# Attention scores as float32 products in 32-row strips, in place of stacked bf16 parts

## The reference

```python
x = x + gamma * attention(layernorm(x), ctx)     # x, ctx: (16, 64, 256)
x = x + ffn(layernorm(x))
# attention: 8 heads of 8 rows each; per batch and head, q, k: [8, 256]
qk  = einsum('dq,dl->ql', q, k) / sqrt(8)        # k = v = ctx, 256 x 256 scores
ret = einsum('ql,dl->dq', softmax(qk, -1), v)
# ffn: activations rounded to 8 bits, weights to -1/0/1, width 256 -> 1024 -> 256
h = silu(bit_linear(x, w_gate)) * bit_linear(x, w_up)
y = bit_linear(rms_norm(h) * ln_weight, w_down)
```

## Time and profile before

| | |
|---|---|
| runs, us | 245.23, 247.96, 244.26 |
| median | 245.23 |
| span of the profiled execution | 248.6 |
| PE, DVE, ACT, POOL busy | 178.4, 151.6, 140.9, 107.3 |

### The profile page before, as it was taken

The page is one execution under the profiler, slowest core; times in us unless marked ns, Lnnn a source line. Parts: engine busy times, 40 slices in busy tenths (PEclk is TensorE's granted clock), DMA queues, the critical chain, the costliest instruction groups (busy, mean ns, idle before and its releaser), DMA issues.

```text
span 248.6 us, 4308 instructions
## 1 busy us (share of the span) xinstructions
PE 178.4 (72%) x1370; PEld 103.8 (42%) x1378; DVE 151.6 (61%) x282; ACT 140.9 (57%) x286; POOL 107.3 (43%) x282
## 2 busy tenths in 40 slices
PE   0006331972988958994999799589979998893793
PEld 0002111540666624662466366245745664441432
DVE  2105840563297974985666989736886769436273
ACT  4110000893466845973568599447856587975432
POOL 3630310406624544734652586436435226626240
PEclk9999999996599997997569999965995699999689
DMA  3599599348201450253026314601540000000000
GB/s 100 139 142 261 126 177 313 115 121 154 63 1 37 118 107 0 56 149 77 1 67 141 75 26 116 135 9 34 142 105 0 5 3 22 7 21 0 22 1 21
DMA packets 15871, 19.95 MB, mean 80 GB/s; under 512 B 2649, under 2 KB 14057, under 8 KB 14697
## 3 DMA queue, kind: packets, MB, share of 16 engines
q1 hardware_dynamic: 15321, 18.89, 31.8%
q10 hardware_dynamic: 528, 0.79, 1.4%
HBM read 15.20 MB, written 4.19 MB: 78 GB/s over the span
## 4 chain that ended last, share of the span: by engine, by line
PE 33%; DMA 14%; DVE 7%; issue 6%; ACT 6%; POOL 4%; SPq 3%; POOLq 0%; ACTq 0%; DVEq 0%
DMA q_stack<-mt 13%; PE psO L463 9%; PE psB L447 7%; PE psA L433 6%; PE psG L565 2%; PE psG L505 2%; ACT probs L594 2%; PE psG L555 2%; POOL hw L325 2%; DVE mneg L736 1%; SPq L333 1%; ACT o_sb L629 1%; SPq L341 1%; DVE wgT L755 1%; DVE w_sb L747 1%
## 5 line engine op out<-in xcount | busy, mean ns | idle before, releaser
L736 DVE TENSOR_REDUCE mneg<-psA 128x2 f32<-128x512 f32 x128 | 82.7, 680 | 46.5 <-PE psA L433 46.4
L594 ACT ACTIVATE probs<-psB 128x512 f32<-128x512 f32 x128 | 74.0, 597 | 39.8 <-PE psB L447 39.7
L433 PE MATMUL psA<-k_stack,q_stack 72*128 72x256 bf16 x256 | 57.9, 319 | 23.1 <-DMA q_stack<-q_scratch 20.7
L447 PE MATMUL psB<-q_stack,k_stack 75*128 75x256 bf16 x256 | 55.2, 303 | 23.8 <-DMA q_stack<-mt 22.0
L463 PE MATMUL psO<-probs,vt 128*32 128x256 f32 x512 | 41.6, 451 | 1.0 <-ACT probs L594 1.0
L433 PEld LDWEIGHTS psA<-k_stack,q_stack 72*128 72x128 bf16 x256 | 23.9, 108 | 43.3 <-issue 30.1
L447 PEld LDWEIGHTS psB<-q_stack,k_stack 75*128 75x128 bf16 x256 | 25.7, 108 | 37.2 <-DMA q_stack<-mt 23.8
L325 POOL TENSOR_TENSOR hw<-h,lnw 128x512 f32<-128x512 f32 x15 | 19.1, 1270 | 39.3 <-DVE h L826 28.0
L463 PEld LDWEIGHTS psO<-probs,vt 128*32 128x32 f32 x512 | 14.8, 121 | 16.9 <-issue 9.9
L815 DVE SCALAR_TENSOR_TENSOR gu<-th,psG 128x512 f32<-128x512 f32 x15 | 10.3, 688 | 9.7 <-ACT th L657 9.7
L657 ACT ACTIVATE th<-psG,tscale 128x512 f32<-128x512 f32 x15 | 10.3, 688 | 9.1 <-PE psG L535 9.0
(11 more groups left out here) (129 smaller groups left out, 268.4 us busy)
## 6 DMA issues: line engine op xcount, KB each, us to landing
q_stack<-q_scratch SPq DMA_DIRECT2D x24, 192.0 KB
k_stack<-k_scratch SPq DMA_DIRECT2D x21, 192.0 KB
q_scratch<-q_parts SPq DMA_DIRECT2D x24, 64.0 KB, 2.1
k_scratch<-k_parts SPq DMA_DIRECT2D x21, 64.0 KB, 2.0
w_sb<-in_L_ffn_w_gate_dram SPq DMA_DIRECT2D x4, 256.0 KB, 8.0
w_sb<-in_L_ffn_w_up_dram SPq DMA_DIRECT2D x4, 256.0 KB, 7.5
w_sb<-in_L_ffn_w_down_dram SPq DMA_DIRECT2D x4, 256.0 KB, 4.1
out_dram<-y_sb SPq DMA_DIRECT2D x8, 128.0 KB, 4.2
```

The costliest lines, as they stand in the source:

```text
L433: mm = pe.matmul(psA[n % A_BANKS][:, qt * L:(qt + 1) * L], q_stack[0:STACK, t % NBUF, bh, qt * P:(qt + 1) * P], k_stack[0:STACK, t % NBUF, ...
L447: mm = pe.matmul(psB[b % 2][:, lt * L:(lt + 1) * L], k_stack[:, t % NBUF, bh, lt * P:(lt + 1) * P], q_stack[:, t % NBUF, bh, :], start=Tru ...
L594: act.activation(probs[:, b % RING, :], psB[b % 2][:, :], ACT.Exp, scale=SCALE).then_inc(s_exp, 1)
L736: dve.tensor_reduce(mneg[:, k % MBUF, QT * (bh % HALF):QT * (bh % HALF + 1)], psA[n % A_BANKS][:, :].rearrange("p (q l) -> p q l", q=QT), ...
```

## The change

There are no stacks and no parts. `q` holds the normalised x in float32, in two copies (`half` 0 and 1), each masked to half of the heads' rows. `cm` holds ctx in float32 in four copies (`j` 0 to 3), each with all rows zero but the 8 of one head in every 32-row strip, and 8 rows that hold a one for the maxima. Both products of a unit contract over one 32-row **strip** of the array (`STRIP` = 32) in float32. A unit n uses strip (n mod 8) // 2, and with `LAG` = 12 product B of the same step uses another strip than product A. Within a step PE's order is A, B, A, B (the two halves of each), behind one group of waits for both banks.

The maxima need no split: PE transposes `mneg` in float32 once for every 4 units (`quad_at` for `half_at`), ACT copies, SP sends 4 rows of 256 into `q`. Stores to DRAM and stack loads go; `cm` for tiles 1 to 7 is cleared by DVE, POOL and ACT once and filled from ctx by 16 transfers at the start; for tile 0 ACT makes it from the loaded ctx. The weights and what is left of x and ctx are issued by ACT at the start and no longer by SP between the tiles. The table of half-steps is moved by some steps throughout.

```diff
-LAG = 14
+LAG = 12
...
-        def load_k(eng, t):
...
-        def load_q(eng, t):
...
+        def clear_cm(eng, j):
+            return eng.tensor_scalar(cm[:, j, 1:T, :], zero[:, 0:1].unsqueeze(2).to_broadcast([P, T - 1, L]), mask[:, one_row(j):one_row(j) + 1], None, ALU.add)
...
+            for j in (0, 2, 1, 3):
+                sp.wait_ge(s_init[j], 1)
+                for i in range(P // STRIP):
+                    rows = slice(STRIP * i + DH * j, STRIP * i + DH * (j + 1))
+                    sp.dma_start(cm[rows, j, 1:T, :], ctx_rows[1:T, rows].rearrange("g p l -> p g l")).then_inc(s_cm[j], DMA)
...
-                    for qt in range(QT):
-                        mm = pe.matmul(psA[n % A_BANKS][:, qt * L:(qt + 1) * L],
-                                       q_stack[0:STACK, t % NBUF, bh, qt * P:(qt + 1) * P],
-                                       k_stack[0:STACK, t % NBUF, bh, :], start=True, stop=True)
-                    mm.then_inc(s_a, 1)
...
+                        if n >= A_BANKS:
+                            pe.wait_ge(s_red, n - A_BANKS + 1)
+                        first = (q[rows, t, half, :], cm[rows, j, t, :])
+                    if 0 <= b < N:
...
+                        if r % GROUP == 0:
+                            pe.wait_ge(s_mrow[r // GROUP], DMA * (2 * t + half + 1))
+                        if b >= 2:
+                            pe.wait_ge(s_exp, b - 1)
+                        second = (cm[rows, j, t, :], q[rows, t, half, :])
                     for qt in range(QT):
+                        if first:
+                            mm = pe.matmul(psA[n % A_BANKS][:, qt * L:(qt + 1) * L], first[0][:, qt * P:(qt + 1) * P],
+                                           first[1], start=True, stop=True)
...
+                        if second:
+                            mm = pe.matmul(psB[b % 2][:, qt * L:(qt + 1) * L], second[0][:, qt * P:(qt + 1) * P],
+                                           second[1], start=True, stop=True)
...
-                k = half_at(m, PE_M)
+                k = quad_at(m, PE_M)
...
-                    pe.wait_ge(s_ms, k + 1)
-                    pe.transpose(banks[BANK_M][0:PARTS * HALF * QT, 0:P // 2].bitcast(BF16),
-                                 m_parts[:, k % 2].rearrange("p c n -> p (c n)"), ident_b[:, :]).then_inc(s_mt, 1)
+                    pe.wait_ge(s_red, GROUP * (k + 1))
+                    pe.transpose(banks[BANK_M][0:GROUP * QT, 0:P], mneg[:, k % MBUF, :], ident[:, :]).then_inc(s_mt, 1)
```

More of the change, by code:

```diff
@@ L216, in build @@
         s_lnw = sem("lnw_loaded")
-        s_rows = sem("rows_of_ones_made")
         s_ident = sem("ident_made")
+        s_mask = sem("masks_made")
+        s_init = [sem(f"cm_cleared{j}") for j in range(4)]
+        s_cm0 = sem("first_cm_made")
+        s_cm = [sem(f"cm_loaded{j}") for j in range(4)]
         s_const = sem("const_made")
@@ L395, in _ @@
+            for m in range(2 * FIRST, 2 * LAST):
+                k = quad_at(m, ACT_M)
                 if k is not None:
[L396 removed]
+                    t, rest = divmod(k, 4)
+                    half, par = divmod(rest, 2)
+                    first = P // 2 * par + DH * (1 - half)
                     sp.wait_ge(s_mtsb, k + 1)
[L398 to L399 removed]
+                    sp.dma_start(q[first:first + P // 2 - DH:2 * DH, t, half, :].rearrange("p (q l) -> p q l", q=QT),
+                                 mt[:, k % 2, :]).then_inc(s_mrow[k % 2], DMA)
```

346 lines of the change are left out of this document (116 added, 230 removed).

## The result

| | before | changed |
|---|---|---|
| runs, us | 245.23, 247.96, 244.26, 250.49 | 309.08, 308.42, 304.48, 321.71 |
| median | 246.59 | 308.75 |
| span of the profiled execution | 248.6 | 307.3 |

The profiled execution of the changed kernel is the one of 309.08 us. The ratio is 1.252, with a 95% interval of 1.216 to 1.288. The forecast was 249 us with a range to 280: outside, and on the wrong side of "no change".

What follows compares the result with a forecast made beforehand. PE was taken to bound the kernel between holes. First `o_sb` at 43, tile 1 31.6, five tiles of 26.2 and a last of 24.0 reach 229.6; with 22.5 after, span 252.1, times 0.986: 249 us, range 229 to 280.

Steps and rivals of the forecast that it cites:

- on a cold clock at first: Start: twelve steps with product A alone, 0.85 to 1.7 us each, taken as 1.05; first B at 19 us.
- if PE then never idles: Tiles: condition for the half clock to go with the 7.8 us transfers, some 6 us a tile together.
- over 45 us a tile: Tiles: length at half clock if 32-row products don't hold the clock; named as making the forecast wrong, given no chance.
- `cm` arrives late: Start: sign that the forecast is wrong, `cm` coming late beside 3 MB of weights in the same engines.
- The tile's sum: One tile on PE: work 22.2 us, 13.65 of it strips (16 x 0.853), shape changes 2.3, waits 1.7; together 26.2.
- a change of shape 0.10: Tile on PE: each switch between strips and other work costs 0.10 us, 23 of them 2.3 us a tile.
- Rival 1: Tiles: shape changes and new waits are covered, 23.7 us a tile, 231 us in all; chance 0.24.
- Rival 2: Steps: the common wait in front makes ACT the pacer, +3.3 us a tile, 274 us; chance 0.20.
- Rival 3: Steps: strips don't overlap, 356 us, or loads don't, a step of 1.41 and 319 us; chance 0.10 together.
- between the holes PE is the bound: Kernel before: without holes and half clock, 16.5 to 17.3 us a tile of work that PE paces.
- the start's 28 us: Start: 28 us won there, then spent at 3.5 to 4 us a tile; break-even is a tile of 25.7 us.
- 0.986: Whole kernel: factor from span to time, turning the forecast span of 252.1 into 249 us.

Runs made afterwards that it cites:

- e6: Changed kernel with product B's waits put behind the step's first product A; 311.95 us, one run.
- e1: Changed kernel with both products contracting over 64 rows in place of 32 (output differs); 285.35 us against 308.75.
- e8: Changed kernel with both the repaired start and products over 64 rows (output differs); 278.96 us, two runs.
- e15: Kernel with the repaired start and 64-row products, made exact by zeros in the other strip's rows of q; 280.89 us, ratio 1.155 to the kernel before.
- e10: Changed kernel with both products contracting over all 128 rows, operands all from cm (output differs); 356.48 us, one run.
- e2: Changed kernel with 36 unread bf16 filler products of 128 rows on PE ahead of the first product; 315.10 us, two runs.
- e4: Changed kernel with its start repaired: ACT issues weights inside its loop, POOL and ACT share clearing cm; 302.78 and 324.59 us.
- e13: Kernel before with product B 18 steps behind product A in place of 14; 240.38 us against 249.77, repeated 243.36 against 246.65 (ratio 0.991).
- e14: Kernel with the repaired start, products of units 0 to 23 over 64 rows and later ones over 32; 335.96 us, one run.
- e3: Changed kernel with a step's products written in the order A, A, B, B; 303.06 us, two runs.
- e5: Kernel before with the transfer of the maxima issued from ACT's queue in place of SP's; 252.53 us against 247.5, ratio 1.024.
- e11: Kernel before with the maxima sent from ACT's queue and the stack loads issued one at a time; 263.14 us against 248.86.

## Why the prediction was wrong

**The step that failed is the clock.** The sum of the start and of every tile was made at full clock, apart from a first product "on a cold clock at first", and the half clock was counted among what the change removes "if PE then never idles". In the kernel before the clock does fall beside the ends of holes: at 94.8, 115.3 and 163.0 us, where the transfers of the maxima landed at 93.8, 116.5 and 162.5. In the changed kernel PE did hardly idle (42.84 busy of 43.10 us) and ran at half clock all the same (629 ns a product, against 374). e6 shows full clock lost under 32-row products with hardly a pause, e1, e8 and e15 show it won within 2 to 5 us of the first product B with 64 rows and kept through the tiles but for two falls of 3.4 us in e1, e10 with 128. I had named that condition as what would make the forecast wrong, and given it no chance among the cases: nothing in the trace of before had products over so few rows, which was a reason for a rival, not for leaving it out. My price for it, over 45 us a tile, wasn't put to the test, since no middle tile ran at half clock throughout; the stretches that nearly did took 43.1 us for a forecast 24, and in e2 and e6 39.8 and 39.6 for the last tile's 24.0.

**The size of it.** 28 to 30 us of the 55 are given back by 64 rows together with the start (e8, e15). The rest, 24.7 us in e8, is 8.7 for the stretch of products A alone at half clock, 6.5 in the first two tiles, 7.0 for five tiles that are 1.4 us longer each (0.8 to 0.9 with 32 rows), and 2.5 at the two ends.

**The start.** "`cm` arrives late" was not it. Two waits I had at nothing: POOL's 4.82 us for a copy of `cm` in front of the reciprocal root (I had named only DVE's copy, at 1.1 to 2.1; it took 2.07), and ACT held in issuing weights. Both were in the order of the changed kernel. With both gone in e4, the first B comes 5.5 us earlier.

**The tile's sum was near.** 26.2 forecast, 27.0 to 27.1 measured at full clock. Of its terms: a step 0.853, measured 0.86; a change of shape 0.10, measured about 0.10 in the gap, and a further 0.105 from the first record of a step to its next (0.32 against 0.21 us), which I had not. That stands only behind a change, so in some 11 of the 16 steps, 1.2 us, more than the 0.8 that is missing: some other term was a little too large, and I haven't tested them apart. Last tile 24.0, measured 24.1.

**Rival 1** (changes covered) didn't come. **Rival 2** (ACT as the pacer) was too big by ten times, e6. **Rival 3** (no overlap of strips, or of loads): false on both counts. The loads last 0.18 us each at full clock and stand under running products of the same strip (in the changed kernel a load of A's from 112.72 to 112.90 us, under the product of A that starts at 112.61 and lasts 0.48). A step takes 0.86 us, not the 1.41 that a load of 0.14 behind each record would have given.

**What was removed.** Right: the waits for the transfer are gone. But e13 shows that they could be had for less, by the lead, with the cheap bf16 products kept: a step's products take PE 0.44 us there against 0.86 in strips. It also shows a second step of the prediction to be wrong, "between the holes PE is the bound": a tile with neither holes nor half clock lasts 21.2 us, not 16.5 to 17.3, so there were not some 6 us a tile to win but 1.3 to 1.7. This was not in the sum for the changed kernel, which was made from PE's work alone. That the 13.65 us a tile of strips are more than even the 6 us stood in it; I let the start's 28 us weigh against them.

**The scale.** 0.986 joined the median of three runs to the span of another. In the changed kernel the profiled execution took 1.8 us more than its span, so the forecast span of 252.1 stands for 254 us; that is 5 of the 60 us by which the forecast missed.

**Open.** What starts a fall of the clock in the middle of a run of 32-row tiles (184.1 us, in e6 at 252.1) and not in others, with the same work in each; e14, e2, e3 and e4 each have four or five such tiles in a row at full clock. Between the profiled runs only the place of the falls differs, and each version was profiled once. And whether 32-row products can be kept at full clock for good by more 128-row work among them; the middle tiles, with their outputs' products and transposes, suggest it, and no experiment isolates it.

## What to carry to other kernels

Price a row strip at the clock that it will have: here products over 32 of the 128 rows ran at half clock (629 ns each) for the first 65 us, PE busy for 42.84 of the last 43.10 before the first `o_sb`, and the same products over 64 rows, half of them zeros, at full clock (376 ns) from 3 us after the first B. Before a change that removes a wait at the cost of PE's time, try to give the wait a longer lead; `LAG` and the numbers that follow from it did that here, but check what stands at the new place, since 17 steps lost where 18 won. Read the duration of one kind of product beside the clock column, above all ahead of the first change that the column shows. And before counting a wait as time to be won, find out what would bound the stretch without it.

## What the runs showed of the hardware that I had not expected

- Rows count for the clock even where a factor is zero in them (e15 against e4: 376 against 629 ns at 35 to 65 us).
- PE isn't bound to program order between row strips: A, A, B, B runs as A, B, A, B (27.2 against 27.0 us a tile). Products over 32 and over 64 rows, in contrast, don't overlap, and take 0.62 us for one product, where A and B side by side take 0.43 for both (e14).
- Products A of two units on different strips overlap too: at half clock, where records of one strip start 0.427 us apart (e2 at 12.6 to 13.8 us) and four of them would be 1.7, a unit with A alone takes 1.5 us over 32 rows (12 units in 25.3 - 7.5, e4). Over 64 it takes 1.8 (28.9 - 7.7, e8).
- An engine that issues large transfers can be held by them: 7.84 us for one of 1 MB on ACT, whose earlier ones took 0.57 and 4.12 us.
- POOL's broadcast addition over 1792 elements takes 4.83 us, DVE's 2.07, ACT's 1.79.
- 12 KB sent beside stack loads of 192 KB each are late on another queue too (15.8 us of waits in e5), and with the loads spread out no less so (20.5 in e11, one profile each).
